# Activation-table loads of ScalarE in instructions of their own, ahead of the waits of their step

## What is computed

```python
xn = _layernorm(x)
x = x + _L0_attn_ref(xn, ...) + _L0_ffn_ref(xn, ...)
xn = _layernorm(x)
x = x + _L1_attn_ref(xn, ...) + _L1_ffn_ref(xn, ...)
```

```python
mid = jax.nn.gelu(jnp.einsum('bsd,edf->bsef', h2, e_w1) + e_b1, approximate=False)
eo = jnp.einsum('bsef,efd->bsed', mid, e_w2) + e_b2
moe = jnp.einsum('bse,bsed->bsd', w, eo)
```

## Time and profile before

| | us |
|---|---|
| median of 3 runs | 761.91 (760.92 to 763.23) |
| the profiled execution | 761.48 |
| its span, first to last instruction | 759.6 |
| PE busy | 716.6 |
| DVE busy | 570.0 |
| ACT busy | 506.2 |
| of that in 63 table loads | 80.9 |

### The profile page before, as it was taken

How to read it: one execution, slowest core, us unless ns; L and a number is a source line. 1 busy time by engine, 2 the same in 40 slices (tenths; PEclk the granted TensorE clock), 3 DMA queues, 4 the chain that set the end, 5 groups by cost and what they waited for, 6 DMA issues and landing times.

```text
span 759.6 us, 15885 instructions
## 1 busy us (share of the span) xinstructions
PE 716.6 (94%) x6222; PEld 389.0 (51%) x6222; DVE 570.0 (75%) x1127; ACT 506.2 (67%) x631; POOL 185.6 (24%) x425
## 2 busy tenths in 40 slices
PE   4779899999999999999999999999999999999997
PEld 2333354767444664554534456557554665633345
DVE  5999997545887867588989867658777375788966
ACT  6277777265785466667788857674786747588882
POOL 5165554011432012003523200021371110010000
PEclk9699999999999999999999999999999999999999
DMA  6144532000222000003222200031031000030101
GB/s 161 48 130 141 158 109 76 17 12 3 56 69 77 3 25 16 19 5 108 69 78 68 60 3 18 3 98 30 5 91 52 9 10 17 3 92 6 34 26 38
DMA packets 42010, 38.76 MB, mean 51 GB/s; under 512 B 14312, under 2 KB 37232, under 8 KB 41712
## 3 DMA queue, kind: packets, MB, share of 16 engines
q1 hardware_dynamic: 40592, 36.17, 16.9%
q10 hardware_dynamic: 1152, 1.05, 0.5%
q0 software_dynamic: 192, 0.52, 0.3%
HBM read 10.47 MB, written 1.44 MB: 16 GB/s over the span
## 4 chain that ended last, share of the span: by engine, by line
PE 72%; ACT 14%; DVE 8%; issue 3%; DMA 2%; POOL 1%; ACTq 1%; SPq 0%; POOLq 0%; DVEq 0%
PE psum L978 17%; PE psum L965 16%; PE psum L917 14%; PE psum L896 8%; PE psum L869 8%; DVE neg_max L535 5%; ACT probs L794 3%; ACT probs L770 3%; PE psum L846 3%; ACT L770 3%; ACT L794 2%; PE psum L874 1%; PE psum L927 1%; ACT k_stack L716 1%; PE psum L849 1%
## 5 line engine op out<-in xcount | busy, mean ns | idle before, releaser
L535 DVE TENSOR_REDUCE neg_max<-psum 128x2 f32<-128x1024 f32 (+2 forms) x320 | 344.8, 1112 | 89.2 <-PE psum L869 45.5
L770 ACT ACTIVATE probs<-psum 128x1024 f32<-128x1024 f32 (+1 forms) x320 | 286.4, 939 | 107.2 <-PE psum L896 105.2
L917 PE MATMUL psum<-probs,v_ones 128*32 128x512 f32 (+3 forms) x1536 | 152.4, 495 | 0.0
L794 ACT ACTIVATE probs<-psum,col 128x512 f32<-128x512 f32 x160 | 99.5, 685 | 51.9 <-PE psum L965 51.2
L869 PE MATMUL psum<-k_stack,q_stack 64*128 64x512 bf16 (+3 forms) x768 | 114.6, 333 | 17.8 <-DMA q_stack<-part 8.1
L978 PE MATMUL psum<-ew,probs 128*128 128x128 f32 x1024 | 129.2, 280 | 0.6 <-ACT probs L794 0.6
L978 PEld LDWEIGHTS psum<-ew,probs 128*128 128x128 f32 x1024 | 120.1, 192 | 18.2 <-issue 13.6
L1063 POOL TENSOR_SCALAR_AFFINE_SELECT probs<-probs 128x512 f32<-128x512 f32 x128 | 82.0, 647 | 190.1 <-ACT probs L770 189.9
L965 PE MATMUL psum<-normed_T_a,ew 128*128 128x512 f32 x256 | 118.9, 601 | 1.0 <-ACT probs L770 0.5
L896 PE MATMUL psum<-q_stack,k_stack 64*128 64x512 bf16 (+3 forms) x768 | 108.5, 328 | 10.6 <-ACT probs L770 4.8
L690 DVE SCALAR_TENSOR_TENSOR acc<-psum,gate,acc 128x128 f32<-128x128 f32 x256 | 71.9, 343 | 28.7 <-PE psum L978 27.0
(11 more groups left out here) (126 smaller groups left out, 523.8 us busy)
## 6 DMA issues: line engine op xcount, KB each, us to landing
q_stack<-part SPq DMA_DIRECT2D x66, 128.0 KB, 2.4
k_stack<-part SPq DMA_DIRECT2D x66, 128.0 KB, 2.4
heads_raw<-head_sums SPq DMA_DIRECT2D x24, 128.0 KB
heads_inv<-inverses SPq DMA_DIRECT2D x12, 256.0 KB, 3.2
ew<-w_expert_in SPq DMA_DIRECT2D x4, 512.0 KB, 5.4
ew<-w_expert_out SPq DMA_DIRECT2D x4, 512.0 KB, 6.1
q_stack<-k_stack SPq DMA_DIRECT2D x14, 128.0 KB, 2.3
q_stack<-maxT SPq DMA_DIRECT2D x48, 32.0 KB, 1.8
```

The source lines that it names most:

```text
L535: eng.tensor_reduce(neg_max[:, q % 2, :, xs[0]:xs[-1] + 1, i], src, AX_X, ALU.max, negate=True).then_inc(vector_done.sem, 1)
L770: eng.activation(dst, src, ACT.Exp, scale=SCALE).then_inc(probs_ready.sem, 1)
L794: ins = eng.activation(probs[:, order.slot[step[:-1]], 2 * k + f, :], two_banks(step)[:, f, :], ACT.Gelu_apprx_tanh if layer else ACT.Gelu ...
L917: ins = eng.matmul(sum_bank[32 * c:32 * c + V_COLS, q0:TILES * P], v_ones[u][:, j, g // 2 * QH + c, col0:col0 + V_COLS], probs[:, order.sl ...
```

## The change

ScalarE's program gets a table of which step kinds need which function, and keeps the name of the last table asked for. At the head of a step that needs another one it issues the load as an instruction of its own, in the program text ahead of the step's waits. Steps that need none (`second`, `values` and so on) keep what is there. The order of all steps stays.

```diff
+            tables = {"scores": ACT.Exp, "gate_exp": ACT.Exp, ("expert_in", 0): ACT.Gelu,
+                      ("expert_in", 1): ACT.Gelu_apprx_tanh}
+            table = None
+
             for step in order.plan:
                 kind, b = step[:2]
+                needed = tables.get(kind, tables.get((kind, step[2]) if len(step) > 2 else None, table))
+                if needed != table:
+                    table = needed
+                    eng.preload_act_table(table)
                 if kind == "clear_keys":
```

## The result

The changed kernel takes 741.67 us (median of 4 runs, 740.59 to 744.76) against 762.01 us; the ratio is 0.974, 95% interval 0.971 to 0.977. The gain is 20.3 us. The forecast was 13.3 us and the range began at 744.0 us, so the direction was right and the size was too small.

The account below looks back on a forecast made before the run. PE was taken to bound the kernel (busy 716.6 of 759.6 us). Pairs gave 13.3 us, tails raised this to 16.9, later waits ate 3.6; 761.48 - 13.3 = 748.2, against the median 748.6 us; range 744.0 to 756.0.

Parts of the forecast that it names:

- 45 loads of 62 move: ScalarE's table loads: 45 stand behind the wait on pair_full and move ahead; the other 17 change nothing.
- the new one: The added 1283 ns load ahead of the first scores, where ScalarE waits 14.46 us for PE: costs nothing.
- the 25 pairs: Loads paired with PE's 28 waits for ScalarE behind them; the smaller of hideable time and PE idle sums to 13.3 us.
- the sum with tails and caps: The 25 pairs with 0.16 us added to each, capped by what the load can hide: 16.9 us.
- the method: At each pair, PE's gain is its stall for ScalarE, tail included, capped by what the load can hide.
- correction of 0.16 us for the modelled tail: PE's idle time is understated as a matmul's tail counts as busy; at 170.06 us, 0.47 us stall against 0.31 shown.
- what is late next: PE runs on to its next wait, DVE's reductions (L535), assumed to eat the 3.6 us that the tails add.
- A: Other waits take the stalls' place from 340 to 440 and 530 to 700 us: 7.4 us left, 754.5 us; chance 0.20.
- B: More than the direct effect through ScalarE's head start, up to all of PE's 20.5 us idle: 741.4 us; chance 0.06.
- C: No measurable change: stalls move whole to later waits, or loads already ran ahead of waits; 761.9 us; chance 0.06.
- D: Slower: a load in its own place holds the ACTIVATE behind it; 766.9 us, or 763.5 with the drain; chance 0.03.

Follow-up runs that it names:

- experiment 1: The changed kernel without its one new load ahead of the first scores, the 62 others as in it: 741.38 us, ratio 0.973 to before.
- experiment 8: The kernel before with only one load moved, that of the first Gelu near 124 us: 761.81 us in one run.
- Experiments 9 and 10: The kernel before and the changed kernel, both with the last query tile's maximum reductions done twice on VectorE: 833.64 us without and 820.67 us with the change.
- experiment 2: The kernel before with only the 32 Gelu loads asked for ahead of the waits, Exp loads left alone: 751.02 us, ratio 0.986 to before.
- experiment 6: The changed kernel with Tanh as the experts' activation, so no table load but the one at the start: 742.6 us, ratio 0.974 to before.
- experiment 5: The changed kernel with a second load, of Sqrt's table, ahead of each of its 63 loads: 784.3 us, ratio 1.029 to before.
- experiments 4: The changed kernel with all loads asked for by name but behind all waits of their step: 773.97 us, ratio 1.015 to before.

## Why the prediction was right in direction and wrong in size

**Right: what bounds, what moves, which stalls go.** PE bounds, 45 loads of 62 move, the new one is free (experiment 1), and most of the gain lies at the 25 pairs. The pairs measured 17.2 us; the sum with tails and caps was 16.9 us. At 126.49, 170.59 and 387.42 us the gaps shrank by 1.28, 0.47 and 1.25 us, where the method gives 1.28, 0.47 and 1.25. The correction of 0.16 us for the modelled tail was right, and PE's busy time bears it out: after 120 us it fell from 619.5 to 613.6 us, 1.6 us of that by the clock, though no matmul was taken away. Over the whole span it fell by 5.1 us (716.6 to 711.5). I had said that it would stay within 3 us, which contradicted my own correction.

**The first term that failed is "what is late next".** I let other waits eat 3.6 us and went back from 16.9 to 13.3 us. Given back were 1.75 us in the trace, and nothing to another engine behind the single stall of experiment 8. That term was 1.85 us too large. The evidence stood in the earlier trace rows: PE waited 0.5 us for the reductions in 640 us. I set the busy share of VectorE in two stretches above it. Experiments 9 and 10 show that it takes a good deal more before the stalls move.

**The second is that the list of stalls was not complete.** I counted gaps in which PE showed 0.15 us or more of idle time with ScalarE named as the releaser. Another 3.2 us were in gaps that showed less, since the modelled tail covers the first 0.16 us, or that named VectorE: 0.31 us at 664.88 us and 0.25 us at 698.26 us. The first of these went whole with the Gelu loads alone (experiment 2), so it had hung on ScalarE all the same. Another 0.5 us are in steps under 0.1 us. So the sum should have been 17.2 + 3.2 + 0.5 - 1.75 = 19.2 us, and the 16.9 us that I called the upper bound of the direct effect was none; the range, built on it, ended at 744.0 us, 2.3 us above the measured time. Another view shows more of it: the waits of PE's weight loads. In the whole span of before, then of the changed kernel:

```profile
PEld psum L896 <- ACT probs L770: 34.0, 53, 1.2
...
PEld psum L869 <- ACT probs L770: 22.8, 38, 1.5
...
PEld psum L869 <- ACT probs L794: 6.1, 7, 1.4
```

```profile
PEld psum L904 <- ACT probs L778: 28.4, 48, 0.8
...
PEld psum L877 <- ACT probs L778: 20.6, 37, 1.2
```

Over all lines from 120 us on, the weight loads' waits for ScalarE were some 67 us before and are 47 us now: 20 us less, with 19.2 us of the change's own gain after 120 us. Most of the 47 us is no stall of PE: with no table load at all (experiment 6) they are 46 us, and no wait of PE's matmuls for ScalarE is listed there after 120 us.

**The rivals.** A fell (0.3 us of PE waits for L535 left). B gave the nearest number, 741.4 us, but hardly by its mechanism: PE's idle time is still 740.0 - 711.5 = 28.5 us, not below the 26 us that I named for it, and the head starts that pass another load are small (0.24 us at 668.04 us). That its number agrees is luck: it took PE's whole idle time of 20.5 us, of which 6.4 us are left (620.0 - 613.6), and the tails, which no idle time shows, happen to make up for the rest. C and D fell; D by experiment 5 and by the load of 1.28 us that ends 1.32 us ahead of its Gelu with all of that time named PE's.

Two expectations behind the prediction missed for a related reason. In experiments 4 and 5 I took PE's share of a change in ScalarE's time from the change itself, 0.49, and it was 0.7 and 0.75. Both 0.49 and 0.75 hold dips of the clock; without them they are 0.45 (19.2 of 42.8 us) and 0.67. The share is no constant even so: 80.8 us off ScalarE beyond the change gave 0 (experiment 6), 42.8 us off before it 0.45, 56.9 us more on it 0.67. The later ScalarE is, the more of each further microsecond reaches PE. That it is one curve for all these places is my reading; it was not tested in smaller steps.

## What to carry to other kernels

Where an instruction needs no data, put it ahead of the waits of the step it serves, and look at the built order to see which ones already stand there. What it gives is what the bounding engine stood still for, place by place; count those gaps from start to start of its instructions, since idle time with a modelled tail leaves out a part of each and nearly all of the small ones. Let later waits eat of that only as much as the bounding engine is seen to wait for others there, not as much as others are busy; and a load with no idle time around it may still be covering a wait, which only shows when it is moved.

## What the runs showed of the hardware

A table load ahead of a wait runs while the engine would have waited, at 1283 ns as everywhere, and the ACTIVATE behind it starts as soon as its wait is over. Two loads back to back take 2 x 1283 ns on ScalarE (experiment 5). The granted clock fell to the lower level from 230.3 to 233.8 us in the profiled run of before, and with the same stalls ahead of it did not in another kernel's run; this one dip was worth 1.6 us, a thirteenth of the difference that I was explaining. Three such dips cost the kernel of experiment 5 some 1.5 us each. The same transfer into `q_stack` took 2.4 us from issue to landing in some profiled runs and 3.8 to 4.4 us in others, and PE waited for it in the latter (experiment 8).
